# Scores of eight head pairs from plain fp32 queries and keys in 32-row groups of the array

## What is computed

```
norm(x, t) = (t@gw.T + gb) * x * rsqrt(mean(x*x) + 1e-6) + (t@bw.T + bb)
q, k, v    = norm1(x, t) @ Wq.T, @ Wk.T, @ Wv.T      # 16 heads of 16 channels
attention  = softmax(q @ k.T / 4) @ v @ Wo.T         # inside one sequence
x1  = x + attention
out = x + x1 + (silu(norm2(x1, t) @ gate.T) * (norm2(x1, t) @ hid.T)) @ out_w.T
```

## Time and profile before

| | |
|---|---|
| median of three runs | 1129.42 us (1127.95 to 1131.92) |
| profiled execution | span 1131.1 us; the profile states no time beside the span |
| PE busy | 1094.5 us, 97% |
| VectorE busy | 752.0 us, 66% |
| ScalarE busy | 427.2 us, 38% |
| GpSimd busy | 304.8 us, 27% |
| DMA | 97.18 MB, of which HBM reads 12.95 MB and writes 8.39 MB |
| mean granted clock of PE | 0.980 |

### The profile page before, as it was taken

One profiled execution on the slowest core, in us unless ns is written; L12 is line 12 of the kernel. 1 busy time (PEld: TensorE's weight loads), 2 busy tenths in 40 slices (PEclk: granted clock), 3 DMA queues, 4 the chain that ended last, 5 costly groups with the idle time before them and its releaser, 6 DMA issues.

```text
span 1131.1 us, 20909 instructions
## 1 busy us (share of the span) xinstructions
PE 1094.5 (97%) x7244; PEld 985.1 (87%) x7244; DVE 752.0 (66%) x1434; ACT 427.2 (38%) x887; POOL 304.8 (27%) x268
## 2 busy tenths in 40 slices
PE   5889999999999999999999999999999999999988
PEld 4778989898998989899898989989898998989876
DVE  4366667676866767686676768667676866767552
ACT  3223343433434343343434334343433434333232
POOL 4041313133231313323131332313133231323222
PEclk9679999999999999999999999999999999999999
DMA  4906244251623425162342516244251623416000
GB/s 149 213 5 126 61 85 122 48 126 31 144 60 83 121 46 124 34 144 60 83 121 46 122 36 144 60 83 121 43 121 39 142 62 83 121 42 144 2 19 19
DMA packets 37400, 97.18 MB, mean 86 GB/s; under 512 B 6784, under 2 KB 24384, under 8 KB 31104
## 3 DMA queue, kind: packets, MB, share of 16 engines
q1 hardware_dynamic: 37152, 96.76, 36.6%
q10 hardware_dynamic: 224, 0.10, 0.0%
HBM read 12.95 MB, written 8.39 MB: 19 GB/s over the span
## 4 chain that ended last, share of the span: by engine, by line
PE 90%; issue 5%; DVE 2%; POOL 1%; DMA 1%; ACT 0%; SPq 0%; POOLq 0%; DVEq 0%
PE ps L834 11%; PE ps L835 10%; PE ps L839 10%; PE ps L733 10%; PE ps L734 10%; PE ps L735 10%; PE ps L823 9%; PE ps L801 9%; PE ps L813 5%; PE ps L748 1%; PE ps L740 1%; PE ps L940 1%; DVE x_scaled L503 1%; PE ps L764 1%; DMA result<-in_modT 0%
## 5 line engine op out<-in xcount | busy, mean ns | idle before, releaser
L296 POOL TENSOR_TENSOR h_lo<-shared,h_hi 128x512 fp32r<-128x512 f32 x128 | 166.8, 1303 | 420.3 <-ACT h_hi L416 420.3
L411 ACT ACTIVATE shared<-ps 128x512 f32<-128x512 f32 x128 | 76.3, 596 | 246.7 <-PE ps L839 246.7
L733 PE MATMUL ps<-out_w_hi,h_hi 128*128 128x256 f32 x512 | 153.0, 299 | 1.4 <-POOL h_lo L296 1.4
L801 PE MATMUL ps<-k_stack,q_stack 96*128 96x64 f32 x1024 | 140.7, 283 | 5.0 <-DMA q_stack<-q_lo 5.0
L735 PE MATMUL ps<-out_w_hi,h_lo 128*128 128x256 f32 x512 | 144.3, 282 | 0.0
L734 PE MATMUL ps<-out_w_lo,h_hi 128*128 128x256 f32 x512 | 144.1, 282 | 0.0
L421 ACT ACTIVATE probsT<-ps 128x512 f32<-128x512 f32 x128 | 76.5, 598 | 172.2 <-PE ps L813 172.2
L801 PEld LDWEIGHTS ps<-k_stack,q_stack 96*128 96x128 f32 x1024 | 131.0, 200 | 5.8 <-DMA q_stack<-q_lo 5.8
L823 PEld LDWEIGHTS ps<-values,probsT 128*128 128x128 f32 x1024 | 130.5, 197 | 3.7 <-issue 1.2
L823 PE MATMUL ps<-values,probsT 128*128 128x66 f32 x1024 | 132.3, 273 | 1.3 <-DVE att L561 0.8
L569 DVE TENSOR_REDUCE row_max<-ps 128x8 f32<-128x512 f32 x128 | 87.7, 685 | 55.0 <-PE ps L801 54.3
(11 more groups left out here) (89 smaller groups left out, 2191.4 us busy)
## 6 DMA issues: line engine op xcount, KB each, us to landing
q_stack<-q_hi SPq DMA_DIRECT2D x128, 256.0 KB, 4.2
k_stack<-k_hi SPq DMA_DIRECT2D x128, 128.0 KB, 2.4
q_stack<-q_lo SPq DMA_DIRECT2D x64, 256.0 KB, 4.6
x_in<-in_x SPq DMA_DIRECT2D x16, 512.0 KB, 3.9
k_stack<-k_lo SPq DMA_DIRECT2D x64, 128.0 KB, 2.4
out<-result SPq DMA_DIRECT2D x15, 512.0 KB, 3.0
shared<-in_attT SPq DMA_DIRECT2D x1, 1024.0 KB, 6.8
shared<-in_gateT SPq DMA_DIRECT2D x1, 1024.0 KB, 8.7
```

Source lines behind the costliest of these rows:

```text
L296: nc.gpsimd.tensor_tensor(h_lo[:, j % 2, :], h[:, :], h_hi[:, j % 2, :].bitcast(F32), ALU.subtract).then_inc(h_lo_done, 1)
L733: nc.tensor.matmul(dst, a_hi, b_hi, start=first, stop=False, skip_group_check=skip)
L801: last = nc.tensor.matmul(ps[:, score_bank(t, p), tok], q_stack[:, r % 2, c, b, :], k_stack[:, r % 2, c, tok], start=True, stop=True)
```

## The change

Queries and keys are kept in plain fp32, in two tiles without high and low parts; half of each is copied from PSUM by ScalarE, half by VectorE. The stacks, their 24 DMAs a tile, and `pair_of` are gone. A score product takes its 32 channels where they lie: pair p in rows 32*(p % 4) to 32*(p % 4) + 31 of half p // 4. Scores are issued for two pairs at once (in tile 0 for four), alternating between pairs, each pair into a bank of its own; a burst waits until the exps of all earlier pairs are done. The transposes of a pair go to the bank from which its scores were read. Some fillers move or go.

```diff
-STACK = 3
-ROUNDS = PAIRS // CH
-FILL_K, FILL_S0, FILL_S1, FILL_STEP = 8, 10, 6, 4
-GATE, HIDDEN, Y, SCORE, TRANS, OUT, EXTRA = 0, 1, 2, 4, 5, 6, 7
+GROUPS = P // ROWS
+TOGETHER, FIRST_TOGETHER = 2, 4
+FILL_K, FILL_STEP = 8, 4
+GATE, HIDDEN, Y, SCORE, OUT, EXTRA = 0, 1, 2, 4, 6, 7
...
+        def together(t):
+            return FIRST_TOGETHER if alone(t) else TOGETHER
         def score_bank(t, p):
-            return GATE if alone(t) and p % 2 else SCORE
+            return (SCORE, SCORE + 1, GATE, HIDDEN)[p % together(t)]
...
-            def high_k(u):
-            def high_q(u, c):
...
+            def first_keys(u):
+                act.wait_ge(k_mm, CH * u + 1)
+                nc.scalar.copy(keys[:, 0, :], ps[:, SCORE, :]).then_inc(k_act_done, 1)
+            def first_queries(u):
+                act.wait_ge(q_mm, CH * u + 1)
+                for head in range(2):
+                    last = nc.scalar.activation(queries[:, 0, :, head, :],
+                                                ps[:, GATE, :].rearrange("p (b q) -> p b q", q=L), ACT.Copy,
+                                                scale=head_mask[:, head:head + 1])
+                last.then_inc(q_act_done, 1)
...
-            def low_k(u):
-            def low_q(u, c):
...
+            def second_keys(u):
+                dve.wait_ge(k_mm, CH * u + 2)
+                nc.vector.tensor_copy(keys[:, 1, :], ps[:, SCORE + 1, :]).then_inc(k_dve_done, 1)
+            def second_queries(u):
+                dve.wait_ge(q_mm, CH * u + 2)
+                for head in range(2):
+                    last = nc.vector.tensor_scalar(
+                        queries[:, 1, :, head, :], ps[:, GATE + 1, :].rearrange("p (b q) -> p b q", q=L),
+                        head_mask[:, head:head + 1], None, ALU.mult)
+                last.then_inc(q_dve_done, 1)
...
-            def scores(t, p):
+            def scores(t, first):
+                if first == 0:
+                    pe.wait_ge(k_act_done, t + 1)
+                    pe.wait_ge(k_dve_done, t + 1)
+                    pe.wait_ge(q_act_done, t + 1)
+                    pe.wait_ge(q_dve_done, t + 1)
+                    pe.wait_ge(v_even, 2 * t + 2)
+                    pe.wait_ge(v_odd, 2 * t + 2)
+                wait(pe, exp_done, PAIRS * t + first)
                 for b in range(SEQS):
                     tok = slice(b * L, (b + 1) * L)
+                    for p in range(first, first + together(t)):
+                        c, rows = p // GROUPS, slice(p % GROUPS * ROWS, p % GROUPS * ROWS + ROWS)
+                        last = nc.tensor.matmul(ps[:, score_bank(t, p), tok],
+                                                queries[rows, c, b, :, :].rearrange("p h q -> p (h q)"),
+                                                keys[rows, c, tok], start=True, stop=True)
+                        if b == SEQS - 1 and p % TOGETHER == TOGETHER - 1:
+                            last.then_inc(score_mm, 1)
...
                 for p in range(PAIRS):
                     if alone(t) and p == 0:
-                        pe.wait_ge(q_lo_done, CH)
-                        keep_clock_up(FILL_S0)
-                        scores(t, 0)
-                    if not alone(t) and attend:
-                        if isinstance(t, int) and t == 1 and p == 0:
-                            pe.wait_ge(q_lo_done, 2 * CH)
-                            keep_clock_up(FILL_S1)
+                        pe.wait_ge(mod_done, 4 * CH)
+                    if attend and p % together(t) == 0:
                         scores(t, p)
-                        if isinstance(t, int) and t == 1 and p < LAG:
-                            keep_clock_up(FILL_STEP)
-                    if alone(t) and p + 1 < PAIRS:
-                        scores(t, p + 1)
+                    if alone(t) or isinstance(t, int) and t == 1 and p < LAG:
                         keep_clock_up(FILL_STEP)
```

More of the change, by code:

```diff
@@ L100, in conditioned_block @@
         xn1_lo = sb("xn1_lo", [P, CH, TOK], F32R)
[L103 to L109, removed]
+        queries = sb("queries", [P, CH, SEQS, 2, L])
+        keys = sb("keys", [P, CH, TOK])
         values = sb("values", [P, BLK, PAIRS, VW])
@@ L201, in _ @@
                          hidT.rearrange("(c p) n -> p c n", p=P)).then_inc(hid_w_in, 16)
[L203 to L227, removed]
             sp.wait_ge(w_split, 3)
@@ L431, in _ @@
             high_weights(1, gate_w_in, 16, gate_w_hi[:, :, :].rearrange("p c n -> p (c n)"), 1)
-            high_k(0)
-            for c in range(CH):
-                high_q(0, c)
+            first_keys(0)
+            first_queries(0)
             for half in range(2):
@@ L561, in normalise @@
                     last = nc.vector.tensor_tensor(
-                        att[rows, :, pair_of(p), :].rearrange("p (k s) d -> p k s d", s=2), own,
+                        att[rows, :, p, :].rearrange("p (k s) d -> p k s d", s=2), own,
                         recip[rows, :].rearrange("p (k s) -> p k s", s=2).unsqueeze(3).to_broadcast([L, BLK, 2, DH]),
@@ L631, in _ @@
             add_biases(1)
-            low_k(0)
-            for c in range(CH):
-                low_q(0, c)
+            second_keys(0)
+            second_queries(0)
             for half in range(2):
@@ L687, in iteration @@
                 if ahead:
[L688 removed]
+                    second_keys(t + 1)
                 if attend:
@@ L691, in iteration @@
                     normalise(t, PAIRS - 1)
-                if ahead:
-                    low_q(t + 1, 0)
                 if attend:
@@ L758, in channel_major, with keep_clock_up @@
                 return last
-            def keep_clock_up(products):
+            def keep_clock_up(products, bank=Y + 1):
                 for n in range(products):
-                    nc.tensor.matmul(ps[:, HIDDEN, :], att_w_hi[:, 0, 0, 0:P],
+                    nc.tensor.matmul(ps[:, bank, :], att_w_hi[:, 0, 0, 0:P],
                                      att_w_hi[:, 1, :, :].rearrange("p c n -> p (c n)"), start=True, stop=True)
@@ L778, in project_v @@
             def project_v(u, half):
-                pe.wait_ge(k_lo_done, CH * u + half + 1)
+                pe.wait_ge((k_act_done, k_dve_done)[half], u + 1)
                 for k in (2 * half, 2 * half + 1):
```

71 lines of the change are left out of this document (12 added, 59 removed).

## The result

The changed kernel takes 1197.98 us (median of four runs, 1194.67 to 1199.46) against 1130.67 us for the kernel before beside it: a ratio of 1.0605, 95% interval 1.0573 to 1.0637. It is slower by 6%. The forecast was 1204 us.

What follows compares the result with a forecast made beforehand. Only PE's own stream was taken to set the time, being busy 97% of the span. Step 2 42, step 3 10, step 7 12, row changes 22 and head -11 gave +75 us: 1204 us against the 1129.4 median, range 1165 to 1265.

Steps and rivals of the forecast that it cites:

- a burst of two pairs costs 1.79, as before: Score products: 32 records of two alternating row groups run two at a time, 1.79 us a burst, no change.
- change of rows: Entry and exit of each 32-row burst stall PE, 0.20 us per switch, 22 us with tile 0.
- step 2, wait for exp 1: Burst of pairs 2 and 3 waits for ScalarE's exp 1: 2.8 us in each of 15 tiles, 42 us.
- step 3, wait for hidden(0): gate_hidden(1) waits for bank GATE, with no scores before it: 0.64 us in 15 tiles, 10 us.
- step 7, lost cover: Without scores PE reaches the transposes awaiting VectorE 0.89 us earlier, their start unchanged: 14 tiles, 12 us.
- head: Scores start 4.7 us earlier, tile 0 gains 5, tile 1 loses fillers worth 1.4: together -11 us.
- none of its steps gets earlier: Step 2: the chain to exp 1 keeps its timing, ending 6.21 us after the transposes of step 0.
- GpSimd holds add_shift back: Step 2: VectorE's add_shift stays held until GpSimd's own L296 is done; it ran 1.45 us beside it.
- All ready: Step 2: down(7), probs_values(1) and gate_hidden(0), behind the waiting burst, were all said to be ready.
- A: Rival: loads of different row groups go one after another, +115 us, about 1319 us; chance 0.12 in full, 0.08 halfway.
- B: Rival: short stalls in steps 2, 3 and 7, no drain at switches: +20, about 1150 us; chance 0.07.
- C: Rival: not slower, short 32-row records make bursts pay for waits; decided at a burst of 0.62 us; chance 0.07.

Runs made afterwards that it cites:

- e4: Changed kernel with the loops over pairs and sequences in a burst exchanged, so one pair's 8 products come before the next pair's: 1346.66 us.
- e1: Changed kernel with the steady tiles' burst of pairs 2 and 3 moved behind down(7) and probs_values(1): 1198.06 us, 71.72 us a tile.
- e5: Changed kernel with probs_values(1) moved in steady tiles from before gate_hidden(0) to behind the transposes of step 2: 1180.49 us.
- e6: Changed kernel with down(4) moved in step 7 ahead of the transposes that wait for VectorE: 1179.85 us.
- e3: Kernel before with score products reading only the first 32 of the 96 stacked rows: 1163.0 us, 67.95 us a tile for 66.06.
- e12: Changed kernel with the same work reordered on PE, ScalarE, GpSimd and VectorE to mend the steady tiles' waits: 1151.64 us, 68.27 us a tile.
- e14: e12 with probs_values put ahead of down in steps 3 and 5: 1126.43 us, 66.83 us a tile.
- e13: e12's order with three score bursts a steady tile in place of four: 1096.81 us, ratio 0.972 to the kernel before.

## Why the prediction was right

The total was right to 6 us, but not by its own terms throughout: two errors of about 20 us had opposite signs. Each over 15 tiles, in us:

| step of the prediction | forecast | trace |
|---|---|---|
| a burst of two pairs costs 1.79, as before | 0 | 0 (e4 shows the other case) |
| change of rows | +22 | +13 |
| step 2, wait for exp 1 | +42 | +23 |
| step 3, wait for hidden(0) | +10 | +9 |
| step 7, lost cover | +12 | +13 (14 tiles) |
| clock at half once a tile | not seen | +24 (15 stretches more) |
| head | -11 | -19 |
| sum | +75 | +63 |

The spans are 61.8 us apart; 1.4 us of the difference are tile 1's six filler products, which the forecast had under the head. The medians are 67.3 us apart.

- **The burst.** The overlap of two row groups is there, and a burst costs what two stacked pairs did. The limit of two at a time was right for two groups; with four, four records run beside each other.
- **Change of rows.** The mechanism read from the prologue was right. The size was off: 0.24 us for entry and exit together at full clock. From 0.30 for each change at half clock I had taken 0.20 for each, 0.40 together. Scaled with the clock it would have been 0.15 each, which is nearer.
- **Step 2.** The wait is at the place named and from the engine named, but 1.56 us for 2.8. Exp 1 ends 4.98 us after the transposes of step 0 (659.35 after 654.37) for the 6.21 forecast. The step that failed is "none of its steps gets earlier", in two parts. VectorE's add_shift starts 3.15 us after these transposes (657.52) where it started 3.61 after them (633.22), 0.46 earlier; before, VectorE had waited 0.28 us for pair 1's scores, which now come with pair 0's. The other 0.76 us is "GpSimd holds add_shift back": this time add_shift came 0.07 us ahead of L256 and took 0.69 us in place of 1.45, and GpSimd's L256 took 1.75 us in place of 1.29. Of these two operations, which slow each other, the first to start kept its pace. "All ready" behind the burst was wrong as well: down(7) was not, as e1 showed.
- **Step 3 and step 7** came out to 0.03 us a tile. e5 and e6 removed them.
- **The clock** was missing. No row of before had a fall in a steady tile, and the sum has no term for it. That its 24 us came near the 19 us overpriced in step 2 is chance, and the forecast was right in its sum partly by that.
- **Head.** The earlier start was worth 7.1 us in this trace (forecast 4.7). The value copies end earlier too, 29.24 for 31.78 us, but with first scores from 27.5 to 34.2 us in the other runs the excess of 2.4 us means little. Tile 0's 11.6 us (forecast 5) were in the bound of 16.
- **Rivals.** A fell in the changed kernel and appeared in e4. B fell: changes of rows cost time (13 us), and the waits of steps 2 and 7 were longer than it had. C fell by its own threshold, 0.62 us for a burst: it took 1.79.

## What to carry to other kernels

A long product that looks like a cost may be another wait's cover: when work moves between steps, count what each next wait still has in front of it, and look on every engine for what stands behind the moved piece. Packing row groups pays where it reduces the number of bursts, not where it replaces equal work; here the same idea went from 6% slower to 3% faster by order and by three groups for two. Read the granted clock by windows after such a change, because it can go to half in each tile while PE shows no idle time, and count these stretches before giving a gain to a wait.

## What the runs showed of the hardware

- Four row groups take records together as cheaply as two: 64 records in 2.0 us, 32 in 2.0 us, 0.112 us for each group's next record; without alternation 32 take 3.3 us.
- A stretch of 32-row products between full-height ones costs 0.24 us at full clock, entry and exit together (e3). With 64 rows at half clock each change costs 0.30 us.
- The granted clock fell to half for 3.4 us once a tile with PE busy 940 of 940 us (e12) and stayed at 1.00 with 881 busy of 940 (e1). Such a stretch cost about 1.57 us. Separating two stretches of small products went with a full clock (e14), but e1 and e13 have them side by side at full clock too. What it answers to stays open.
- VectorE's add_shift took 0.69 us and GpSimd's L256 1.75 us where VectorE was 0.07 us ahead; with GpSimd 0.38 us ahead it was 1.45 and 1.29 us.
